# Tokens' load moved within SyncE's order, eight tiles per expert loop body, and null rows written as 15 whole-row DMAs

## The reference, cut to what matters

```python
x = x + _L0_conv_ref(_ln_c(x), qkv_w, rpb, proj_w, proj_b)   # attention over 7x7 neighbours
t = _to_tokens(x)                                            # 25088 tokens of 128 channels
# experts, on n = _ln_t(t):
logits = n @ W_router; topk_p, topk_i = top_k(softmax(logits), 2)
for e in range(E):                                           # E = 8, hidden width 512
    out = out + combine[:, e:e+1] * (relu(n @ W1[e] + b1[e]) @ W2[e] + b2[e])
x = _from_tokens(t + out)
```

## Time and profile before

| what | value |
|---|---|
| median of 3 runs | 3335.22 us (3326.73 to 3337.24) |
| the profiled execution, own time | 3327.84 us |
| its span in the trace | 3326.0 us |
| mean granted PE clock, share of full speed | 0.885 |
| PE busy | 2640.0 us (79%) |
| POOL busy | 2337.5 us (70%) |
| DVE busy | 2310.5 us (69%) |
| ACT busy | 2161.6 us (65%) |
| DMA engines, mean share of the dynamic queues | about 46% |

### The profile page before, as it was taken

The page is one execution under the profiler, slowest core; times in us unless marked ns, Lnnn a source line. Parts: engine busy times, 40 slices in busy tenths (PEclk is TensorE's granted clock), DMA queues, the critical chain, the costliest instruction groups (busy, mean ns, idle before and its releaser), DMA issues. The chain is left out here.

```text
span 3326.0 us, 119405 instructions
## 1 busy us (share of the span) xinstructions
PE 2640.0 (79%) x35139; PEld 2225.8 (67%) x35140; DVE 2310.5 (69%) x12691; ACT 2161.6 (65%) x5836; POOL 2337.5 (70%) x2809
## 2 busy tenths in 40 slices
PE   4778888888888888888888888888708999999833
PEld 2677777777777777777777777777605666666522
DVE  2677777777777777777777777788735656665544
ACT  1567777777777777777777777777616666666500
POOL 2468888788888888888888878888825666666600
PEclk9888898898988899898888888898859999999955
DMA  1444444444444444444444444445243334333399
GB/s 43 141 122 121 122 120 121 117 122 121 120 121 120 121 122 120 122 128 119 119 120 120 118 117 122 123 124 123 82 86 75 87 83 87 84 87 83 79 299 321
DMA packets 638218, 397.75 MB, mean 120 GB/s; under 512 B 417139, under 2 KB 595603, under 8 KB 637654
## 3 DMA queue, kind: packets, MB, share of 16 engines
q1 hardware_dynamic: 584854, 254.86, 33.4%
q10 hardware_dynamic: 24192, 81.67, 7.6%
q0 software_dynamic: 28608, 54.48, 5.0%
HBM read 232.92 MB, written 117.53 MB: 105 GB/s over the span
## 5 line engine op out<-in xcount | busy, mean ns | idle before, releaser
L905 POOL TENSOR_TENSOR pl<-pt 100x512 f16<-100x512 f32 x784 | 815.7, 1040 | 363.4 <-ACT pt L1013 362.1
L1005 ACT ACTIVATE pr<-sc,nmx 128x100 f32<-128x100 f32 x3136 | 921.4, 367 | 86.6 <-DVE nmx L669 82.1
L669 DVE CUSTOM_DVE_ANT_0 sc<-bank,near 128x100 f32<-128x100 f32 x3136 | 630.3, 256 | 350.9 <-PE bank L487 324.3
L487 PE MATMUL bank<-kimg,qexp 128*128 (+2 forms) x9408 | 673.9, 225 | 48.0 <-issue 31.1
L1013 ACT ACTIVATE pt<-bank 100x512 f32<-100x512 f32 x784 | 461.7, 589 | 347.7 <-PE bank L513 342.2
L487 PEld LDWEIGHTS bank<-kimg,qexp 128*128 128x128 bf16 (+1 forms) x9408 | 587.1, 105 | 113.3 <-issue 81.3
L1388 POOL DMA_INDIRECT yrows<-ye,meta x420 | 428.8, 1021 | 280.6 <-DVE ye L1348 170.5
L513 PE MATMUL bank<-vwin,pt 100*128 100x65 bf16 (+1 forms) x6272 | 427.2, 201 | 124.9 <-DVE om L699 79.6
L496 PE MATMUL bank<-cst_sb,pr 128*100 128x128 f32 x3136 | 522.7, 294 | 0.0
L513 PEld LDWEIGHTS bank<-vwin,pt 100*128 100x128 bf16 x6272 | 389.4, 104 | 190.7 <-issue 95.6
L911 POOL TENSOR_TENSOR oml<-om 128x256 f16<-128x256 f32 x784 | 484.3, 618 | 22.6 <-issue 5.9
(11 more groups left out here) (151 smaller groups left out, 4802.5 us busy)
## 6 DMA issues: line engine op xcount, KB each, us to landing
vwin<-v_rows SPq DMA_DIRECT2D x112, 705.5 KB
near<-bias_rows ACTq DMA_DIRECT2D x112, 600.0 KB
v_rows<-vrow SPq DMA_DIRECT2D x560, 48.4 KB
y<-yrows SPq DMA_DIRECT2D x112, 224.0 KB, 4.6
qexp<-qring SPq DMA_DIRECT2D x896, 14.0 KB
xin<-in_x SPq DMA_DIRECT2D x56, 224.0 KB
xres<-in_x SPq DMA_DIRECT2D x112, 112.0 KB
x<-xres SPq DMA_DIRECT2D x112, 112.0 KB
```

The source lines that it names most:

```text
L487: mm = pe.matmul(ps_s[m % 2][:, 2 * t + blk, :], a_, b_, start=n == 0, stop=n == 2)
L669: i = v.tensor_tensor_reduce(out=sc[:, ring(m, par), k, :], in0=ps_s[m % 2][:, k, :], in1=near[:, st, ct, k, :], scale=-1.0, scalar=-MASKE ...
L905: g.tensor_tensor(pl[:, m % 2], pt[:, m % 2], pt_h[:, m % 2], ALU.subtract).then_inc(s["t_out"], 1)
L1005: i = a.activation(pr[:, r, k, :], sc[:, r, k, :], ACT.Exp, bias=nmx[:, r, k:k + 1], scale=-1.0)
```

## The change

Three edits. In the attention block `load_tokens(J - 1)` is called right behind the second `load_res`, ahead of `windows(J + 1, 0)` and of `store_v`. In the expert block the loops of all engines run over eight tiles per turn; `meta` becomes a ring of eight with eight semaphores, `xT` and `ye` stay rings of four; SP loads `xT` after the wait for the first layer of tile i - 4 alone, and waits for the scatter of tile i - 8 ahead of `meta`. The null rows are made as whole rows of 130 words in a larger SBUF tensor (15 x 4 x 130 words per partition), and each group goes out in one DMA; the seven dummy groups are issued behind `null_done`, ahead of any wait for the tables, the other eight behind the first step of the tables.

```diff
+                    if not early(J, 1):
+                        load_tokens(J - 1, 1 - par)
                     if more:
                         windows(J + 1, 0, tail)
                     if I is not None:
                         store_v(I)
-                    if not early(J, 1):
-                        load_tokens(J - 1, 1 - par)
...
-        null = sb("null", [128, 4, C])
-        nulld = sb("nulld", [128, E + DUMMY, 4, 2], I32)
+        null = sb("null", [128, E + DUMMY, 4, C + 2], I32)
...
-        meta = sb("meta", [128, XR, 4, 2])
+        meta = sb("meta", [128, MR, 4, 2])
...
             def moe_tiles(eng, body):
-                for i in range(4):
+                for i in range(MR):
                     body(i, i)
-                with eng.Fori(4, NT - 4, 4) as i:
-                    for r in range(4):
+                with eng.Fori(MR, NT - MR, MR) as i:
+                    for r in range(MR):
                         body(i + r, r)
                 body(NT - 1, 0)
...
+                def put_null(at_, k):
+                    sp.dma_start(xrows[at_, :].rearrange("(g p) w -> p g w", p=128), null[:, k]).then_inc(s["null_in"], 16)
                 sp.wait_ge(s["null_done"], 2)
-                sp.wait_ge(s["t_ready"], 3)
-                def put_null(at_, k):
-                    dst = xrows[at_, :].rearrange("(g p) w -> p g w", p=128)
-                    sp.dma_start(dst[:, :, 0:C], nulli).then_inc(s["null_in"], 16)
-                    sp.dma_start(dst[:, :, C:C + 2], nulld[:, k]).then_inc(s["null_in"], 16)
+                for k in range(DUMMY):
+                    put_null(slice(E * CAP + k * T, E * CAP + k * T + T), E + k)
+                sp.wait_ge(s["t_ready"], 1)
                 for e in range(E):
                     put_null(bass.ds(sp.value_load(n_tab[0:1, e:e + 1], min_val=0, max_val=E * CAP), T), e)
-                for k in range(DUMMY):
-                    put_null(slice(E * CAP + k * T, E * CAP + k * T + T), E + k)
-                sp.wait_ge(s["null_in"], 32 * (E + DUMMY))
+                sp.wait_ge(s["t_ready"], 3)
+                sp.wait_ge(s["null_in"], 16 * (E + DUMMY))
...
                     if not early(i, XR):
                         sp.wait_ge(s["m_hpre"], FC * (i - XR) + FC)
-                        sp.wait_ge(s[f"m_sc{r}"], 16 * 4 * (i // XR))
+                    sp.dma_start_transpose(xT[:, r % XR], xrows[bass.ds(at_, T), 0:C].bitcast(BF16)).then_inc(s[f"m_x{r % XR}"], 16)
+                    if not early(i, MR):
+                        sp.wait_ge(s[f"m_sc{r % XR}"], 16 * 4 * ((i - MR) // XR) + 16 * 4)
                     sp.dma_start(meta[:, r].bitcast(I32), xrows[bass.ds(at_, T), C:C + 2].rearrange("(g p) w -> p g w", p=128))\
                         .then_inc(s[f"m_meta{r}"], 16)
-                    sp.dma_start_transpose(xT[:, r], xrows[bass.ds(at_, T), 0:C].bitcast(BF16)).then_inc(s[f"m_x{r}"], 16)
```

More of the change, by code:

```diff
@@ L62 @@
 XR = 4
+MR = 8
 ZR = 4
@@ L1143, in build @@
         oo = sb("oo", [C, 2, TOK])
-        nulli = null[:].bitcast(I32)
         c_names = """w2_in split_h split1 split2 b2_in b2_step b2_ready w_small
-            null_done null_in t_step t_ready m_x0 m_x1 m_x2 m_x3 m_meta0 m_meta1 m_meta2 m_meta3 m_hpre m_hf m_hh m_hl m_y m_ye m_sc0 m_sc1 m_sc2 m_sc3
+            null_done null_in t_step t_ready m_x0 m_x1 m_x2 m_x3 m_meta0 m_meta1 m_meta2 m_meta3 m_meta4 m_meta5 m_meta6 m_meta7 m_hpre m_hf m_hh m_hl m_y m_ye m_sc0 m_sc1 m_sc2 m_sc3
             z_x0 z_x1 z_x2 z_x3 z_sum z_t z_out z_store0 z_store1""".split()
@@ L1156, in moe_tiles @@
             def moe_tiles(eng, body):
-                for i in range(4):
+                for i in range(MR):
                     body(i, i)
-                with eng.Fori(4, NT - 4, 4) as i:
-                    for r in range(4):
+                with eng.Fori(MR, NT - MR, MR) as i:
+                    for r in range(MR):
                         body(i + r, r)
                 body(NT - 1, 0)
+            assert NT % MR == 1
             def out_tiles(eng, body):
@@ L1228, in first @@
                 def first(i, r, e):
-                    pe.wait_ge(s[f"m_x{r}"], 16 * (i // XR) + 16)
+                    pe.wait_ge(s[f"m_x{r % XR}"], 16 * (i // XR) + 16)
                     for f in range(FC):
@@ L1234, in first @@
                         for n, (a_, part) in enumerate(((w1h, 0), (w1h, 1), (w1l, 0))):
-                            mm = pe.matmul(ps_h[f][:, :], a_[:, w], xT[:, r, part, :], start=n == 0, stop=n == 2)
+                            mm = pe.matmul(ps_h[f][:, :], a_[:, w], xT[:, r % XR, part, :], start=n == 0, stop=n == 2)
                         mm.then_inc(s["m_hpre"], 1)
@@ L1259, in moe @@
                         before = pe.value_load(e_tab[0:1, bass.ds(i - 1, 1)], min_val=0, max_val=E - 1)
-                        second(i - 1, (r - 1) % 4, before)
+                        second(i - 1, (r - 1) % MR, before)
                 moe_tiles(pe, moe)
@@ L1344, in gated @@
                     v.wait_ge(s["m_y"], i + 1)
-                    v.wait_ge(s[f"m_meta{r}"], 16 * (i // XR) + 16)
+                    v.wait_ge(s[f"m_meta{r}"], 16 * (i // MR) + 16)
                     if not early(i, XR):
-                        v.wait_ge(s[f"m_sc{r}"], 16 * 4 * (i // XR))
-                    v.tensor_tensor(ye[:, r], ps_y[r % 2].rearrange("p (g c) -> p g c", c=C),
+                        v.wait_ge(s[f"m_sc{r % XR}"], 16 * 4 * (i // XR))
+                    v.tensor_tensor(ye[:, r % XR], ps_y[r % 2].rearrange("p (g c) -> p g c", c=C),
                                     meta[:, r, :, 0:1].to_broadcast([128, 4, C]), ALU.mult).then_inc(s["m_ye"], 1)
@@ L1353, in moe @@
                     if not early(i, 1):
-                        gated(i - 1, (r - 1) % 4)
+                        gated(i - 1, (r - 1) % MR)
                 moe_tiles(v, moe)
@@ L1379, in _ @@
             def _(g):
-                g.memset(nulld[:], 0)
-                g.memset(null[:], 0.0).then_inc(s["null_done"], 1)
+                g.memset(null[:], 0).then_inc(s["null_done"], 1)
                 g.wait_ge(s["null_done"], 1)
-                g.tensor_copy(nulld[:].rearrange("p k g w -> p (k g) w")[:, :, 1:2], tcol("ndest", 4 * (E + DUMMY)).unsqueeze(2)).then_inc(s["null_done"], 1)
+                g.tensor_copy(null[:].rearrange("p k g w -> p (k g) w")[:, :, C + 1:C + 2], tcol("ndest", 4 * (E + DUMMY)).unsqueeze(2)).then_inc(s["null_done"], 1)
                 def spread(i, r):
@@ L1388, in spread @@
                         g.indirect_dma_start(out=yrows, out_offset=bass.IndirectOffsetOnAxis(ap=meta[:, r, q, 1:2].bitcast(U32), axis=0),
-                                             in_=ye[:, r, q, :], in_offset=None).then_inc(s[f"m_sc{r}"], 16)
+                                             in_=ye[:, r % XR, q, :], in_offset=None).then_inc(s[f"m_sc{r % XR}"], 16)
                 moe_tiles(g, spread)
```

## The result

| | before | changed |
|---|---|---|
| median of 4 runs beside each other, us | 3330.97 (3312.22 to 3337.24) | 3208.56 (3194.47 to 3212.63) |
| ratio | | 0.9634, 95% interval 0.9583 to 0.9685 |
| profiled execution, us (its span) | 3327.8 (3326.0) | 3212.63 (3210.4) |
| body of the attention loop, us | 41.29 | 40.21 |
| end of the attention block, us | 2450.1 | 2390.9 |

3110 us were forecast, 3045 to 3205 was the range: the direction was right, the time lies 3.6 us above the range. The spans differ by 115.6 us, and they split into attention 59, null rows 11, tiles 55, and the last stage, which became 10 us longer: 59 + 11 + 55 - 10 = 115. The tiles and the null rows came as forecast. Attention was to give 152 and gave 59.

A forecast was written before the change was run, and what follows sets the result against it. It took PE's wait for the tokens' load, paid as idle time and again at half clock, to hold attention: 3327.8 - 152 (attention) - 11 (null rows) - 57 (tiles) = 3107.8, stated as 3110 us, range 3045 to 3205.

The forecast's parts named there:

- What bounds the kernel: Attention: PE waits 139.0 us, 44 times, before r_turn for the tokens' load, then works at half clock.
- floor (b): Attention: SP cannot turn a body faster than 37.7 us; its 53.0 us of landings over eight bodies stay.
- rival 1: Attention: compute decides, not SP; bodies about 36.5 us, 3025 us in all; SP's landings may shrink; chance 0.13.
- The windows have half a body of slack: Attention: windows(J + 1, 0), issued 0.4 to 0.5 us later behind the moved load, has slack enough.
- rival 2: Attention: PE idles 1.5 to 2 us per body for windows(J, 1); bodies near 39.8, 3180 us; chance 0.18.
- the compute floor (a): Attention: estimate of 36 to 37.5 us per body from compute, with POOL needing 33.8 us of pure work.
- The null rows: Stretch ahead of the first xT: a larger memset of about 8.1 us stays hidden, 15 issues replace 30; gain 11 us.
- the queue's bound: Null rows: 4.0 MB at 179 GB/s takes 22 us, with xT at 2483, a gain of 11 us.
- The tiles: Expert tiles: lifting the xT wait brings 5.67 us per tile; gain 57 us with the ramp, ends 40 and 63.
- The loop of eight: Expert tiles: PE's doubled code is taken as kept, so the longer loop's jumps cost 0.
- The clock: Attention: a granted clock of 0.97 or above was named as a sign that the forecast is right.

The follow-up runs named there:

- x3: The changed kernel with windows(J, 1) issued ahead of the first store and its landing wait; 3177.0 us, ratio 0.9509.
- x15: The changed kernel with 30 always-met waits added to SP's stream in every attention body; 3499.41 us, ratio 1.0089.
- x5: The changed kernel with SP's order rearranged so that its waits for landed stores fall behind other issues; 3122.6 us, ratio 0.9346.
- x12: The changed kernel with windows(J, 1) right behind spread_q, strip stores after it, POOL's scatters spread and a 1920-byte spacer; 3306.28 us, ratio 0.9455.
- x8: The changed kernel with the xT load again waiting for the scatter of tile i - 4, loop of eight kept; 3283.35 us.
- x16: The same kernel as x12, timed again on another chip with slow tiles; 3284.44 us, ratio 0.9465.
- runs 13 to 16: Set made together on one slow-tile chip: the kernel before (3468.17 us), the changed kernel (x14), x15 and x16.
- x9: The changed kernel unaltered, timed beside x10 on a chip with slow tiles; 3442.84 us, ratio 0.9848.
- x10: The changed kernel with an unused tensor of 1920 bytes per partition behind meta, moving later buffers; 3428.55 us, ratio 0.9794.
- x14: The changed kernel unaltered, on the same chip as x15; 3418.75 us, ratio 0.9867.

## Why the prediction was half right

**What bounds the kernel.** Right: PE's wait at `r_turn` and the half clock behind it were a stall of every body, and both went: 5.1 us in two units.

**Attention, floor (b).** This step failed. It took 41.29 - 3.6 = 37.7 us as SP's turn, by subtracting all of SP's waits for compute and holding its 53.0 us of landings to be fixed. The landings were the half that was off. Per body the trace of before has 31.0 us of issue, 6.2 of landings, 2.5 for `vrow` and 1.25 for `xres`, 0.3 for the rest. With the waits for compute gone (x3) the landings are 7.8 and the issues 31.4, so the turn is 39.5, not 37.7. In its own order the changed kernel stood at 40.21, with 1.5 us per body of waiting for compute still left. The prediction's rival 1 had thought that the landings might shrink; they grew. The length of the body is not the reason, as x15 shows: its bodies are the longest, 42.1 us, and from the store to the load behind it SP stands 8.0 us per body there, 7.6 to 7.9 in the changed kernel's three traces and 6.6 before. Nearly all of the growth is at the store that stands right behind the windows' load: 4.7 us before, 5.8 in the changed kernel, while the other store has 1.9 and 1.8. In x3, where the windows' load goes ahead of the first store, that one has 6.1 and the second 2.1. So the landing is long behind 705 KB of traffic; why it is 1.1 us longer in the changed kernel than before was not tested.

**Attention, the slack of the windows.** "The windows have half a body of slack" was said of `windows(J + 1, 0)`, and no run speaks against it there. `windows(J, 1)`, whose place is behind a store, its landing and a load, had none once the tokens' wait was gone: before, it arrived in time (4.5 us of such waits in 45 bodies) while PE was held up by the tokens earlier in the same body. That is rival 2, which had chance 0.18 and said 3180 us at bodies of 39.8; it came out as 3208.56 at 40.21. Its mechanism is the one that was found, with 79.0 us of such waiting in about 47 bodies, or 1.7 us in each, where it said 1.5 to 2; its size was short by 0.4 us per body, or 20 us, and the last stage's 10 us make the rest. It should have been the forecast: the one line for `vwin` in the earlier trace rows was the clue to which load had no slack.

**Attention, the compute floor (a).** 36 to 37.5 us was a little low: with SP relieved (x5, x12) bodies are 38.1 to 38.2, with POOL's `pl` as PE's releaser in x5. The estimate was taken from bodies without the loop's jump and added nothing for it; without the bodies that end with a jump, x12 is at 37.65.

**The null rows.** The sum was right, 10.9 us for 11, but in part by luck. The memset took 6.60 us for the 8.1 taken, hidden as said behind SP's loads until 2398.2; the 15 issues took 16.91 us where the queue's bound said 22, and the landing 8.3 where the sum left 2.5, and the two misses nearly cancel. The stretch is not the same in every run either: 43.1 to 46.8 us in the kernels with the old null rows, 32.1 to 35.6 in those with the new.

**The tiles.** Right: 55.4 us for 57, 5.67 us a tile for 5.67. The loop of eight cost nothing, as taken, which x8 separates. This holds for chips with quick tiles; on the other kind the one pair that was traced gained nothing.

**The last stage.** Not looked at, and worth -10 us. The change moved buffers by 28800 bytes, and the diff shows this: it alters the sizes of `null` and `meta`, ahead of `xo` and `oo` in the order of allocation.

**The clock.** 0.97 was named and 0.92 came. By the granted clock in the trace, 21.0% of attention from 300 to 2150 us ran at 1.2 GHz before, 15.7% in the changed kernel, 13.1% in x3, 8.6% in x5 and 6.6% in x16: it fell with PE's stalls. It also differs between chips: on that of runs 13 to 16 it was 17.0% before and 13.1% in the changed kernel.

## What to carry over

Before a wait is removed, list for the engine that feeds it, a DMA queue's issuer above all, how much of its turn is issue and how much is landings of its own work: that sum is its floor, the landings change with the order, and only a run in which it waits for no one shows it whole. What arrives in time now may do so only because the reader is held up elsewhere, so look at the load with the least slack behind the removed wait. And an edit to a buffer's size moves every buffer behind it: pad it and time the stages that use them; here a move by 30720 bytes, a multiple of 2048, cost nothing and one by 28800 cost 10 to 18 us.

## What was not expected of the hardware

- The wait for a store's landing is no constant. It is 6.2 us per body before, 7.2 in the changed kernel and 7.8 in x3, each with its own order of SP. Right behind a load of 705 KB a store holds SP up for 4.7 to 6.1 us, elsewhere for 1.8 to 2.1. Putting other issues between store and load brings the sum to 3.2 (x5).
- Buffers moved by 28800 bytes instead of 30720 cost a stage full of DMA 8%: 174.0 against 160.9 us, and 100.9 against 92.9 ns for a packet of 1792 bytes (x9, x10).
- On two chips PE pauses for half a microsecond between matmuls of the expert tiles; an edit that gains 55 us where the tiles are quick gained nothing on the one of them where it was traced.
- Waits that are already met cost SP time: 30 of them took it 1.6 us, some 0.05 us each, and as SP is the floor of the body they cost the kernel 2.4% (x15 against x14: 3499.41 / 3418.75 = 1.024).
- A loop's jump back in attention lengthens the last unit of that body from about 3 to 7.5 us (x12), 0.5 us per body over a turn of eight.
